# Layer 2 of a two-layer kernel as seven block products behind a whole batch of layer 1

## The reference

```python
def reference(x, condB_coeff, itok, mask, W0, b0, W1, b1, lora_A, lora_B):
    # layer 1; x is (8, 256, 1024), mask (8, 1024, 1024) of 0 and 1
    out0 = einsum('bsi,oi->bso', x, W0) + b0
    diff = einsum('bsi,bio->bso', x, 2 * mask - 1)
    x = x + out0 + diff * condB_coeff[:, None, None]
    # layer 2; A = lora_A[itok] is (8, 16, 1024), B = lora_B[itok] is (8, 1024, 16)
    out1 = einsum('bsd,od->bso', x, W1) + b1
    h = einsum('bsd,brd->bsr', x, A)
    return x + out1 + einsum('bsr,bor->bso', h, B)
```

## Time and profile before

| | |
|---|---|
| median of 3 runs | 411.49 us (410.44 to 413.1) |
| the profiled execution | 411.09 us, its span 409.3 us |
| TensorE matmuls, weight loads | 2358 and 2358, busy 396.6 and 364.1 us |
| DVE, ACT, POOL busy | 283.1, 183.8, 27.4 us |
| granted TensorE clock | 1.00 on the mean |

### The profile page before, as it was taken

One profiled execution on the slowest core, in us unless ns is written; L12 is line 12 of the kernel. 1 busy time (PEld: TensorE's weight loads), 2 busy tenths in 40 slices (PEclk: granted clock), 3 DMA queues, 4 the chain that ended last, 5 costly groups with the idle time before them and its releaser, 6 DMA issues.

```text
span 409.3 us, 6109 instructions
## 1 busy us (share of the span) xinstructions
PE 396.6 (97%) x2358; PEld 364.1 (89%) x2358; DVE 283.1 (69%) x343; ACT 183.8 (45%) x294; POOL 27.4 (7%) x42
## 2 busy tenths in 40 slices
PE   4899999999999999999999999999999999999995
PEld 3787788899999999999999999999999999999994
DVE  1667978867876688577886679575986679575622
ACT  3565675543444344344444345353444334353322
POOL 2224121000001000010001000010001000000000
PEclk9999999999999999999999999999999999999999
DMA  8999986259531893159531893249731793246002
GB/s 282 267 284 270 272 220 172 73 151 254 150 102 57 200 246 98 58 141 246 166 103 56 200 217 110 75 129 216 200 98 49 197 232 107 88 130 168 0 2 103
DMA packets 93633, 63.33 MB, mean 155 GB/s; under 512 B 3612, under 2 KB 90916, under 8 KB 93605
## 3 DMA queue, kind: packets, MB, share of 16 engines
q1 hardware_dynamic: 93586, 62.95, 58.3%
q10 hardware_dynamic: 18, 0.00, 0.0%
HBM read 51.39 MB, written 8.39 MB: 146 GB/s over the span
## 4 chain that ended last, share of the span: by engine, by line
PE 95%; DMA 2%; SPq 1%; DVE 1%; issue 0%; POOL 0%; ACT 0%; DVEq 0%
PE ps L756 29%; PE ps L758 15%; PE ps L802 13%; PE ps L801 13%; PE ps L800 13%; PE ps L734 4%; DMA w0raw<-in_L_cond_W_dram 2%; PE ps L780 2%; PE ps L778 2%; PE ps L779 2%; PE ps L829 2%; PE ps L766 1%; PE ps L811 0%; DVE wm L589 0%; POOL w0raw L341 0%
## 5 line engine op out<-in xcount | busy, mean ns | idle before, releaser
L756 PE MATMUL ps<-xhl,whi 128*128 128x512 f32 x512 | 184.8, 399 | 0.0
L758 PE MATMUL ps<-xhl,wlo 128*128 128x256 f32 x512 | 143.4, 280 | 0.0
L756 PEld LDWEIGHTS ps<-xhl,whi 128*128 128x128 f32 x512 | 96.5, 188 | 20.0 <-DVE xhl L579 0.4
L800 PE MATMUL ps<-w1hi,yhl 128*128 128x344 f32 (+1 forms) x336 | 108.1, 322 | 0.0
L802 PE MATMUL ps<-w1hi,yhl 128*128 128x344 f32 (+1 forms) x336 | 107.7, 321 | 0.0
L801 PE MATMUL ps<-w1lo,yhl 128*128 128x344 f32 (+1 forms) x336 | 107.6, 320 | 0.0
L596 DVE SCALAR_TENSOR_TENSOR wlo<-wm,cs_minus,whi 128x1024 fp32r<-128x1024 f32 x64 | 81.6, 1274 | 25.3 <-ACT whi L421 25.2
L758 PEld LDWEIGHTS ps<-xhl,wlo 128*128 128x128 f32 x512 | 97.0, 189 | 0.3
L421 ACT ACTIVATE whi<-wm,cs_minus 128x1024 fp32r<-128x1024 f32 x64 | 73.7, 1152 | 43.0 <-DVE wm L589 42.9
L589 DVE SCALAR_TENSOR_TENSOR wm<-wm,cs_twice,w0t 128x1024 f32<-128x1024 int32 x64 | 83.8, 1310 | 10.3 <-ACT w0t L402 8.4
L447 ACT ACTIVATE ysum<-ps,b0col 128x256 f32<-128x256 f32 x64 | 30.3, 474 | 85.5 <-PE ps L758 85.3
(11 more groups left out here) (68 smaller groups left out, 217.3 us busy)
## 6 DMA issues: line engine op xcount, KB each, us to landing
wm<-in_mask_Bx4096x_ik_dram SPq DMA_DIRECT2D x64, 512.0 KB, 4.4
xraw<-in_x_dram SPq DMA_DIRECT2D x28, 256.0 KB, 5.8
w0raw<-in_L_cond_W_dram SPq DMA_DIRECT2D x8, 512.0 KB, 7.2
w1raw<-_L_cond_base_weight_dram SPq DMA_DIRECT2D x8, 512.0 KB, 7.4
out_dram<-zst SPq DMA_DIRECT2D x20, 172.0 KB, 2.1
bt<-bhl SPq DMA_DIRECT2D x48, 64.0 KB, 2.3
out_dram<-zst SPq DMA_DIRECT2D x8, 176.0 KB, 2.2
out_dram<-zst SPq DMA_DIRECT2D x8, 164.0 KB, 2.2
```

Of the source, the lines that this page charges most:

```text
L756: nc.tensor.matmul(ps[:, bank, :], whi[:, s, k, :], xhl[:, b % 2, k, :], start=(k == 0), stop=False, skip_group_check=True)
L758: op = nc.tensor.matmul(ps[:, bank, 0:S], wlo[:, s, k, :], xhl[:, b % 2, k, 0:S], start=False, stop=(k == KT - 1), skip_group_check=True)
L800: nc.tensor.matmul(dst, hi, w1hi[:, c, cols], start=(c == 0), stop=False, skip_group_check=True)
```

## The change

Layer 2 of a batch is now done as a whole, while layer 1 of the next batch runs. Rows and y's columns and W1's columns are halved, and the four quarters of the result come from seven products of half size in place of eight: `product(name, b)` with P1 to P7. Each product has four steps i, of three matmuls of 512 columns (L1374, L1375, L1382). Their operands are y's quarters (`yab`) or sums of them (`ys`: D, S2, S1, S4, made by POOL in `make_d`, `make_s2`, `make_s1`, `make_s4`, split by ACT and DVE), and W1's blocks B11, B21, B22 or sums of them T1 to T4 (`wt`, made once by DVE and POOL, split by ACT, DVE and POOL). The results are summed in PSUM and in `zst` (`read_x`, `sum_c11`, `sum_u3_p5`, `sum_c22`, `sum_c12`). The adapter's A is no longer beside W1: `adapter` (L1305) multiplies the y part that a step has as its weights with 32 or 16 columns of A, in P1 for both row halves and in P2, P4 and P7 for one.

Layer 1 takes three matmuls of 256 columns for each k (x's high part, x's low part, and `wlo` with the high part), and `wlo` is written over `wm`. The low part of x is now POOL's work from batch 2 on (`rows_lo`). Wm has three buffers in place of four, and a mask waits for `l1_done` of the chunk three back. A's and B's parts and four tiles of W1 that have no room are stored in DRAM and loaded again for each batch (`store_a`, `load_at`, `load_tile`). At the start layer 1 of batch 0 and chunks 8 and 9 run before any product; at the end six products of batch 7 are left.

```diff
             def load_mask(n):
-                s = n % MS
-                if n >= MS:
-                    sp.wait_ge(w_lo, n - MS + 1)
+                if n >= KT:
+                    sp.wait_ge(l1_done, (n - MS if n >= KT + MS else n - KT) + 1)
                 src = mask[b].rearrange("(p k) o -> p k o", k=KT)[:, :, c * P:(c + 1) * P]
-                dst = wm[:, s, :].bitcast(I32).rearrange("p (k o) -> p k o", k=KT)
-                sp.dma_start(dst, src).then_inc(mask_in[s], 16)
-
...
+            def store_a():
+                sp.wait_ge(a_lo, 2)
+                sp.dma_start(a_parts.rearrange("e p f -> p e f"), xbuf[:, :, 0, :].bitcast(F32)).then_inc(a_stored, 16)
...
+            def load_at(b):
+                if b == 0:
+                    sp.wait_ge(a_stored, 16)
+                else:
+                    sp.wait_ge(h_done, 2 * b)
+                sp.dma_start(at[:, :, :, :].bitcast(F32), a_parts[b].rearrange("p (k t r) -> p k t r", k=KT, t=2)).then_inc(at_in, 16)
...
+            def make_t2(i):
+                pool.wait_ge(raw["T1"], i + 1)
...
+                nc.gpsimd.tensor_tensor(raw_tile("T2", i), raw_tile("B22", i), raw_tile("T1", i),
+                                        ALU.subtract).then_inc(raw["T2"], 1)
...
+                if i == 0:
+                    pool.wait_ge(x_sum, 1)
...
+                nc.gpsimd.tensor_tensor(half, half, tile("B21", i, 0).bitcast(F32), ALU.add).then_inc(raw["T4"], 1)
...
+            def rows_lo(b, g):
+                pool.wait_ge(x_hi, x_split(b, g))
+                k = slice(g * KH, (g + 1) * KH)
+                nc.gpsimd.tensor_tensor(xbuf[:, k, lo_half(b), :], xt[:, k, lo_half(b), :], xbuf[:, k, 1, :].bitcast(F32), ALU.subtract).then_inc(x_lo, 1)
...
+            def make_s2(b):
+                pool.wait_ge(y_made, KT * b + 8)
+                pool.wait_ge(s_lo, 4 * b + split["D"])
+                nc.gpsimd.tensor_tensor(sum_raw("S2"), sum_raw("D"), yraw[:, KH:KT, P:2 * P], ALU.add).then_inc(s_made, 1)
...
-                    nc.tensor.matmul(ps[:, bank, :], whi[:, s, k, :], xhl[:, b % 2, k, :],
-                                     start=(k == 0), stop=False, skip_group_check=True)
-                    op = nc.tensor.matmul(ps[:, bank, 0:S], wlo[:, s, k, :], xhl[:, b % 2, k, 0:S],
-                                          start=False, stop=(k == KT - 1), skip_group_check=True)
...
+                    nc.tensor.matmul(out_y, whi_chunk(n)[:, k, :], xbuf[:, k, 1, :], start=(k == 0), stop=False, skip_group_check=True)
+                    nc.tensor.matmul(out_y, whi_chunk(n)[:, k, :], xbuf[:, k, lo_half(b), :], start=False, stop=False, skip_group_check=True)
+                    op = nc.tensor.matmul(out_y, lo[:, k, :], xbuf[:, k, 1, :], start=False, stop=(k == KT - 1), skip_group_check=True)
...
-            def layer2(n, st, j):
-                b, c = divmod(n, KT)
...
-                nc.tensor.matmul(dst, hi, w1hi[:, c, cols], start=(c == 0), stop=False, skip_group_check=True)
-                nc.tensor.matmul(dst, hi, w1lo[:, c, cols], start=False, stop=False, skip_group_check=True)
-                op = nc.tensor.matmul(dst, lo, w1hi[:, c, cols], start=False, stop=(c == KT - 1), skip_group_check=True)
...
+            def layer1_x_hi(b):
...
+                    if k % KH == 0:
+                        pe.wait_ge(x_hi, x_split(b, k // KH))
+                    for w in (whi_chunk(n), lo):
+                        nc.tensor.matmul(ps[:, l1_bank(n), 0:S], w[:, k, :], xbuf[:, k, 1, :],
+                                         start=(k == 0 and w is not lo), stop=False, skip_group_check=True)
...
+            def layer1_x_lo(b):
...
+            def adapter(y_part, t, i, rows, first):
+
+                for st in rows:
+                    op = nc.tensor.matmul(ps[:, HB, 2 * R * st:2 * R * st + 2 * R - R * t], y_part,
+                                          at[:, i, 0:2 - t, :].rearrange("p t r -> p (t r)"),
+                                          start=(first and st == rows[0]), stop=False, skip_group_check=True)
+                return op
...
+            def product(name, b):
+                bank = {"P2": V, "P5": Y, "P3": Y}.get(name, X)
...
+                    else:
+                        pe.wait_ge(raw["T1"], KH)
+                elif name == "P2":
+                    if b > 0:
+                        pe.wait_ge(z_dve, 4 * (b - 1) + 1)
+                        pe.wait_ge(first_in, 32 * b)
+                    else:
+                        pe.wait_ge(a_lo, 2)
+                        pe.wait_ge(at_in, 16)
+                        pe.wait_ge(raw["B22"], KH)
...
+                        pe.wait_ge(second_in, 32 * b)
+                if b == 0:
+                    pe.wait_ge(tile_lo[BLOCKS[name]], KH)
...
+                        hi, lo = (ys[:, i, 2 * t + (name in ("P5", "P7")), :] for t in range(2))
+                    t_hi, t_lo = (tile(BLOCKS[name], i, t, b) for t in range(2))
+                    nc.tensor.matmul(ps[:, bank, :], hi, t_hi, start=(i == 0 and name in ("P1", "P2", "P5")), stop=False, skip_group_check=True)
+                    nc.tensor.matmul(ps[:, bank, :], hi, t_lo, start=False, stop=False, skip_group_check=True)
+                    ka = i + KH * (name in ("P2", "P4"))
+                    if rows:
+                        adapter(hi, 0, ka, rows, i == 0 and name == ("P1" if b > 0 else "P2"))
+                        op = adapter(lo, 1, ka, rows, False)
+                        if i == KH - 1 and name in ("P2" if b > 0 else "P1", "P4"):
+                            op.then_inc(h_done, 1)
+                    op = nc.tensor.matmul(ps[:, bank, :], lo, t_hi, start=False, stop=(i == KH - 1), skip_group_check=True)
...
+            product("P2", 0)
+            product("P1", 0)
+            layer1(10, range(0, 8))
+            layer1(11, range(0, 8))
+            layer1(12, range(0, 8))
+            turn_b()
+            product("P6", 0)
+            turn_h(0, 0)
+            product("P7", 0)
+            layer1(13, range(0, 8))
+            product("P4", 0)
+            layer1(14, range(0, 8))
+            turn_h(0, 1)
+            finish(0, 0)
+            layer1(15, range(0, 8))
+            finish(0, 2)
+            product("P5", 0)
+            product("P1", 1)
+            finish(0, 3)
...
+            for b in range(2, NB):
+                layer1_x_hi(b)
+                product("P2", b - 1)
+                layer1_x_lo(b)
+                layer1(KT * b + 1, range(0, 4))
+                turn_h(b - 1, 0)
+                layer1(KT * b + 1, range(4, 8))
+                product("P6", b - 1)
+                layer1(KT * b + 2, range(0, 4))
+                layer1(KT * b + 2, range(4, 8))
+                product("P7", b - 1)
+                layer1(KT * b + 3, range(0, 4))
+                product("P4", b - 1)
+                layer1(KT * b + 3, range(4, 8))
+                layer1(KT * b + 4, range(0, 4))
+                layer1(KT * b + 4, range(4, 8))
+                turn_h(b - 1, 1)
+                layer1(KT * b + 5, range(0, 4))
+                finish(b - 1, 0)
+                layer1(KT * b + 5, range(4, 8))
+                product("P5", b - 1)
+                layer1(KT * b + 6, range(0, 4))
+                finish(b - 1, 2)
+                layer1(KT * b + 6, range(4, 8))
+                product("P1", b)
+                layer1(KT * b + 7, range(0, 4))
+                layer1(KT * b + 7, range(4, 8))
+                finish(b - 1, 3)
+                product("P3", b - 1)
+                finish(b - 1, 1)
+            product("P2", 7)
+            product("P6", 7)
+            turn_h(7, 0)
```

More of the change, by code:

```diff
@@ L61, in x_split, with w1_turned @@
+    place = {}
+    for name, first, tiles in (("B21", 0, 4), ("B11", 4, 3), ("B22", 7, 4), ("T3", 11, 3), ("T1", 14, 4), ("T2", 18, 4), ("T4", 22, 4)):
+        for i in range(tiles):
+            place[name, i] = first + i
+    place["B11", 3] = place["B21", 3]
+    place["T3", 3] = place["B22", 3]
+    kept = ("B21", "B11", "B22", "T3")
+    w1_order = (4, 5, 6, 7, 0, 1, 2, 3)
+    W1S = 5
+    def w1_turned(c, h):
+        return 2 * w1_order.index(c) + h + 1
     def x_split(b, g):
-        return 4 + 2 * (b - 1) + 2 - g
@@ L698, in _ @@
[L698 to L700 removed]
+            make_w(4)
+            chunk_lo(3)
+            make_w(5)
+            chunk_lo(4)
+            make_w(6)
+            chunk_lo(5)
+            chunk_lo(6)
+            make_w(7)
+            sum_lo("D", 0)
+            y_parts_lo(1)
+            chunk_lo(7)
+            make_w(8)
+            make_w(9)
+            chunk_lo(8)
+            y_parts_lo(2)
+            first_rows_lo(1, 0, 0)
```

1640 lines of the change are left out of this document (1041 added, 599 removed).

## The result

| | before | after |
|---|---|---|
| median | 412.1 us (410.44 to 413.1, 4 runs) | 469.15 us (466.21 to 470.62, 4 runs) |
| profiled execution, its span | 411.09, 409.3 us | 469.98, 468.0 us |
| TensorE matmuls, busy | 2358, 396.6 us | 2754, 427.3 us |
| DVE, ACT, POOL busy | 283.1, 183.8, 27.4 us | 334.1, 207.4, 138.6 us |
| granted TensorE clock, mean | 1.00 | 0.96 |

The changed kernel is slower by a ratio of 1.139, 95% interval 1.133 to 1.144. The prediction said slower and 443 us, range 418 to 460. The sign was right, the size was 26 us short, and the time lies outside the range.

A forecast was written before the change was run, and what follows sets the result against it. TensorE was taken to bound the main loop. Its work of 399.8 us, waits of 24.9, 6, 3 and 3, and 4.6 behind the last matmul gave a 441.3 us span; with 1.8 around it, 443 us, range 418 to 460.

The forecast's parts named there:

- Short matmuls: Adapter A's 320 matmuls on TensorE: each costs one bare weight load, 0.11 us, 35.2 us in all.
- first rival: Adapter's short matmuls cost only their columns: 31.7 us less, 411, or 402 with no waits in the loops; chance 0.1.
- 256-column matmuls: Layer 1 on TensorE: 1536 of them, 179.2 us as before, difference 0, bounds 0 and a few us.
- The start: Before P2 of batch 0: P2 starts at about 71 us, TensorE having waited 24.9; bounds 66 and 75.
- The stage with W1's sums: From 71 to about 125 us: TensorE waits 6 us at P4 for tile T4, bounds 0 and 12.
- The main loop: P6 waits for S2 from POOL: 0.5 us in each of six batches, 3 us, bounds 0 and 17.
- second rival: DVE and POOL become the main loop's bound, 3 us uncovered in each of six batches: 458 us; chance 0.12.
- The range: Whole kernel: from 418 us, short matmuls at half a load and some waits gone, to 460 us.
- The end: Batch 7's six products stand alone: 3 us of waiting, bounds 1 and 5, and 4.6 behind the last matmul.

The follow-up runs named there:

- experiment 10: Changed kernel with one short matmul in P1 writing both row halves in place of two, 64 fewer in all: 461.76 us, ratio 1.121.
- experiment 5: Kernel before the change, with layer 1's 512-column matmul split into two of 256 columns: 416.99 us against 412.64, ratio 1.010.
- Experiment 4: Changed kernel with POOL's twenty operations on W1's tiles turned into one-input copies: 458.76 us, ratio 1.114.
- the last kernel of 11: Changed kernel with POOL's loop and W1 tile operations on DVE, P1's short matmuls merged, `sum_c12` between x's low parts: 429.49 us, ratio 1.042.
- experiment 8: Changed kernel with 14 matmuls of 256 columns put in front of P2's wait for `y_lo` in six batches: 468.51 us, ratio 1.135.
- experiment 1: Changed kernel with x's low parts moved from POOL to DVE, ahead of the chunk: 462.66 us, ratio 1.122.

## Why the prediction was right in sign and wrong in size

- **Short matmuls: right.** 0.11 us each taken, 0.11 to 0.12 read, 0.115 from experiment 10. The first rival (nearly free) is out. The ground given against it, that no load starts ahead of the matmul in front of it, can be read in the earlier trace rows, not in the earlier trace rows, which show no loads. The Trainium skill (TensorE: Matmul & The Clock Gate, Back-to-back issue gap) gives about 81 ns for a matmul with its load in a stream at 128 columns. The trace does not agree: here a matmul of 16 or 32 columns takes 0.11 to 0.12 us.
- **256-column matmuls: slightly low.** "Difference 0; bounds 0 and a few us": it was the upper bound, 4 us by experiment 5. I had seen that 0.116 stood close above a load's 0.11 and took the lucky side.
- **The start: 5 us too late.** P2 of batch 0 began at 65.67, the lower bound. The queue was as counted; the rate of 275 GB/s was low, since the first three slices show 296, 342 and 318; and the last to come was y's low part, not `at`.
- **The stage with W1's sums: the waits were mis-sized.** "I take 6 ... bounds 0 and 12". From P2 at 65.67 to the loop at 129.5 are 63.8 us against 48 of work, so 15.8 on top of it: waiting, and matmuls at a clock of 0.67. The mechanism was the one named, and I had its price from the earlier trace rows. I spent it on POOL only ("ten of them wait 1.0") and let DVE keep 0.68 for a tile. Taking turns costs both: DVE lost 1.1 us in each meeting, and DVE was full. Experiment 4 gives 10 of them back, and the last kernel of 11 needs 52.7 us for the stage.
- **The main loop: the step that failed.** "I take 0.5 us for each of six batches, 3; bounds 0 and 17." Work was 47.9 as against 47.6, and 4.0 a batch came on top, the waits for DVE and the slow matmuls behind them. P2 of batch 7 starts at 441.19, so the six batches took 311.7 in place of 288.6: 23.1 us, where the whole span is 26.7 over its forecast. (The stage adds 10, the early start takes 5 off and the end 1.4.) The sum was made for one chain only, S2 up to P6. It did not ask what else DVE has to deliver in the same ten us: y's low part, due at once and placed beside 5.3 us of POOL, and `wm_lo` of the next chunk. The second rival named the cause (DVE and POOL) at 458, "44 of 47.6", and gave it a chance of 0.12; it looked at a whole batch, where there seems to be room, while the room is not where the work is due.
- **The range** took that rival's guess of 3 us a batch as its end. With the waits of the loop (17) and of the stage (12) at their own upper bounds it would have ended at 463, nearer and still short.
- **The end** held: 26.8 us behind the loop, 28.2 predicted.
- The clock was not priced; in the loop that cost nothing, by experiment 8. For the stage it is open.

That the change loses even without these waits was right too: with every wait on the port gone and 64 short matmuls fewer, 429.5 us is still 4% behind the kernel before. No version here beats it.

Not settled: how much of experiment 1's remainder was the port and how much the masks behind `sum_c12`, which stands late there too.
